# Projecting queries and keys behind the third value call of a turn, in a fused attention and FFN layer on one core

## The reference

```python
x = L0_attn_x                      # (32, 256, 128)
xn = _layernorm(x, axis=-1)
# attention: 16 heads of 8 channels
q = einsum('bsd,hde->bhse', xn, wq) + bq      # k and v in the same way
scores = softmax(einsum('bhse,bhte->bhst', q, k) * 8 ** -0.5)
att = einsum('bhst,bhte->bhse', scores, v)    # heads side by side again
attention = att @ wo.T + bo
# feed-forward, with the token before mixed in
xr = mu_r * xn + (1 - mu_r) * xn_prev         # xk in the same way
ffn = sigmoid(xr @ W_r.T) * (square(relu(xk @ W_k.T)) @ W_v.T)
return x + attention + ffn
```

## Time and profile before

| | us |
|---|---|
| median of 3 runs | 479.34 |
| lowest and highest run | 477.69, 480.9 |
| the profiled execution's own time | 477.82 |
| its span | 476.0 |

### The profile page before, as it was taken

The page is one execution under the profiler, slowest core; times in us unless marked ns, Lnnn a source line. Parts: engine busy times, 40 slices in busy tenths (PEclk is TensorE's granted clock), DMA queues, the critical chain, the costliest instruction groups (busy, mean ns, idle before and its releaser), DMA issues. The chain is left out here.

```text
span 476.0 us, 15644 instructions
## 1 busy us (share of the span) xinstructions
PE 444.1 (93%) x5238; PEld 272.0 (57%) x5238; DVE 402.4 (85%) x823; ACT 393.3 (83%) x866; POOL 367.9 (77%) x675
## 2 busy tenths in 40 slices
PE   5698999999999999999999999999999999999994
PEld 4244656565656656565666566566655565666541
DVE  7488898888989998899999888899998889988920
ACT  2047988989888898989888889898898898988883
POOL 6577888888878898788888888788897888876321
PEclk8579999999999999999999999999999999999998
DMA  4444355454344544453455454344554443445100
GB/s 142 134 125 125 104 147 157 127 147 141 111 122 145 156 141 138 121 145 113 127 154 149 139 148 124 102 142 135 156 154 124 149 127 111 129 135 147 47 15 22
DMA packets 85836, 60.42 MB, mean 127 GB/s; under 512 B 6192, under 2 KB 73392, under 8 KB 85808
## 3 DMA queue, kind: packets, MB, share of 16 engines
q1 hardware_dynamic: 85808, 60.06, 44.1%
HBM read 29.89 MB, written 29.36 MB: 124 GB/s over the span
## 5 line engine op out<-in xcount | busy, mean ns | idle before, releaser
L524 DVE TENSOR_REDUCE neg_max<-bank_max 128x2 f32<-128x512 f32 x512 | 328.2, 684 | 44.6 <-PE bank_max L645 40.1
L425 ACT ACTIVATE probs<-bank_exp 128x512 f32<-128x512 f32 x512 | 278.7, 600 | 25.4 <-PE bank_exp L635 24.1
L635 PE MATMUL bank_exp<-ops 51*128 51x256 bf16 x1024 | 156.9, 272 | 4.1 <-issue 3.0
L645 PE MATMUL bank_max<-ops 48*128 48x256 bf16 x1024 | 159.2, 276 | 0.0
L584 PE MATMUL bank_val<-probs,val 128*25 128x256 f32 x2048 | 138.1, 383 | 1.2 <-ACT probs L425 1.2
L635 PEld LDWEIGHTS bank_exp<-ops 51*128 51x128 bf16 x1024 | 75.0, 94 | 77.0 <-issue 65.2
L584 PEld LDWEIGHTS bank_val<-probs,val 128*25 128x25 f32 x2048 | 55.8, 103 | 41.6 <-issue 20.2
L645 PEld LDWEIGHTS bank_max<-ops 48*128 48x128 bf16 x1024 | 76.4, 95 | 5.2
L335 POOL TENSOR_SCALAR xn<-x_in,moments,rstd 128x128 f32<-128x128 f32 x62 | 49.4, 804 | 0.0
L374 POOL TENSOR_TENSOR mixed_x<-mixed_x,xn_t 128x512 f32<-128x512 f32 x32 | 40.7, 1272 | 2.5
L386 POOL TENSOR_TENSOR y<-projected,rest 128x256 f32<-128x256 f32 x32 | 23.4, 732 | 21.7 <-ACT projected L458 21.7
(11 more groups left out here) (67 smaller groups left out, 635.1 us busy)
## 6 DMA issues: line engine op xcount, KB each, us to landing
ops<-spill SPq DMA_DIRECT2D x128, 192.0 KB, 3.4
spill<-qk_h SPq DMA_DIRECT2D x64, 192.0 KB, 3.3
spill<-qk_m SPq DMA_DIRECT2D x64, 128.0 KB, 2.0
x_in<-x SPq DMA_DIRECT2D x32, 128.0 KB, 2.2
spill<-qk_l SPq DMA_DIRECT2D x32, 128.0 KB, 1.8
y_out<-y SPq DMA_DIRECT2D x32, 128.0 KB, 1.9
ops<-shift SPq DMA_DIRECT2D x128, 6.0 KB
w<-weights SPq DMA_DIRECT2D x1, 448.0 KB, 3.2
```

The costliest lines, as they stand in the source:

```text
L425: nc.scalar.activation(probs[g % 2][:, u % G, :, :], bank_exp[u % 2][:, :, :], ACT.Exp, scale=SCALE).then_inc(exp_done[u], 1)
L524: nc.vector.tensor_reduce(out=neg_max[hf][:, :, r, pr], in_=bank_max[MAX_BANK[v]][:, :, :], axis=AX_X, op=ALU.max, negate=True).then_inc(m ...
L635: exp_mm = nc.tensor.matmul(bank_exp[r][:, i, :], ops[p][rows, hf, 1, pr, i * P:(i + 1) * P], ops[p][rows, hf, 0, pr, :], start=True, stop ...
L645: max_mm = nc.tensor.matmul(bank_max[MAX_BANK[v]][:, i, :], of[rows, max_hf, 0, max_pr, i * P:(i + 1) * P], of[rows, max_hf, 1, max_pr, :] ...
```

## The change

The call of `project` moves from behind u 15 to behind u 13 of PE's program, directly behind value call 2. The key and query copies of ACT move from the head of the next turn to behind the exponential of u 13, so ahead of that of u 14, and name sample `t+3`. The ReLU `act_r` goes from behind the exponential of u 13 to behind that of u 11, after `projected`. DVE takes the keys' remainder behind the reduction of u 14, where it was u 15, and the queries' behind that of u 15, where it was u 1 of the next turn. As the copies are now in the turn of the projection, `near` and `far` swap in their calls. SP's and POOL's programs stay as they are.

```diff
--- before.py
+++ after.py
@@ -403,19 +403,16 @@
                 nc.scalar.copy(shift[half][:, :], shift_in_bank(bank)).then_inc(shift_done[half], 1)
 
             def move_qk(a, bank, n, moved):
-                act.wait_ge(qk_psum[a], n(2))
-                after(act, qk_rest_done[a], n(1))
+                act.wait_ge(qk_psum[a], n(3))
+                after(act, qk_rest_done[a], n(2))
                 if a == 1:
-                    after(act, spill_done, moved(1, SPILLS))
+                    after(act, spill_done, moved(2, SPILLS))
                 nc.scalar.activation(qk_h[:, a, :], bank[:, 0:S], ACT.Identity,
                                      bias=col[:, C_BQ + a:C_BQ + a + 1]).then_inc(h_done[a], 1)
 
             def step(t, c, n, moved, paired, quad, live):
                 p = c % 2
                 near, far = misc[p], misc[1 - p]
-                if live(2):
-                    move_qk(1, near, n, moved)
-                    move_qk(0, far, n, moved)
                 for u in range(H):
                     if live(0):
                         g = u // G
@@ -456,9 +453,12 @@
                         act.wait_ge(wo_psum, n(-1))
                         after(act, y_done, n(-2))
                         nc.scalar.copy(projected[:, :], near[:, 0:ST * D]).then_inc(wo_done, 1)
-                    if u == 13 and live(1):
+                    if u == 11 and live(1):
                         after(act, act_sq_done, n(0))
                         nc.scalar.activation(act_r[:, :], far[:, S:2 * S], ACT.Relu).then_inc(act_r_done, 1)
+                    if u == 13 and live(3):
+                        move_qk(1, far, n, moved)
+                        move_qk(0, near, n, moved)
 
             steps(act, step, (2, SPILLS))
 
@@ -523,10 +523,6 @@
                             after(dve, max_split[hf], n(ahead - 1))
                         nc.vector.tensor_reduce(out=neg_max[hf][:, :, r, pr], in_=bank_max[MAX_BANK[v]][:, :, :], axis=AX_X,
                                                 op=ALU.max, negate=True).then_inc(max_done[v], 1)
-                    if u == 1 and live(2):
-                        take_high(0, far, n(2), n(1))
-                        if not live(1):
-                            split_first()
                     if u == 5 and live(-1):
                         dve.wait_ge(tokens_psum, n(-1))
                         nc.vector.reciprocal(inv_den[:, :], by_head[:, :, E]).then_inc(inv_done, 1)
@@ -559,8 +555,12 @@
                         dve.wait_ge(weights_in, 16 * N_WEIGHT_DMAS)
                         dve.wait_ge(ident_made, 1)
                         fill_constants()
+                    if u == 14 and live(3):
+                        take_high(1, far, n(3), n(2))
                     if u == 15 and live(3):
-                        take_high(1, far, n(3), n(2))
+                        take_high(0, near, n(3), n(2))
+                        if not live(2):
+                            split_first()
 
             steps(dve, step, (SPILLS,))
 
@@ -724,7 +724,7 @@
                         last.then_inc(wo_psum, 1)
                     if u == 13 and live(0):
                         mix_values(2, n(0), n(-1), p)
-                    if u == 15 and live(3) and (live(1) or not live(2)):
+                    if u == 13 and live(3) and (live(1) or not live(2)):
                         project(c, n, live)
 
             steps(pe, step, (2,))
```

## The result

| | before | after |
|---|---|---|
| median, us | 478.51 (4 runs, 477.43 to 480.9) | 491.84 (4 runs, 491.14 to 493.56) |
| ratio, 95% interval | | 1.027 (1.023 to 1.032) |
| span of the profiled execution | 476.0 | 491.8 |

The change makes the kernel 2.7% slower, 13.3 us by the medians. The prediction was a loss of 8.6 us, 487.9 us in a range of 481.0 to 495.0.

A forecast was written before the change was run, and what follows sets the result against it. PE, busy 444.1 of 476.0 us, was taken to bound the kernel. Value call 2 to u 2 grows from 4.61 to 4.94 us; 0.33 x 29 = 9.6, less 1.0, gives 8.6 us: 487.9 us, range 481.0 to 495.0.

The forecast's parts named there:

- The stall on two exponential banks: At u 0 and 1, PE waits for the exponentials of u 14 and 15; u 14 to u 2 takes 2.96 us.
- The queries' copy: On ACT, it stands ahead of the exponential of u 14 and delays it by 0.09 us, bounds 0 and 0.25.
- the maxima's 0.05: At u 0 and 1, maxima matmuls, absent at the end of the trace, add 0.05 us behind the wait.
- The seams: On PE behind value call 2, joining the projection to the stretch saves 0.23 us a turn, 0.84 instead of 1.07.
- DVE's burst: Behind u 14, DVE takes maxima and remainders in a row; PE at u 3 and 4 barely doesn't wait.
- Rival C: DVE's run of work makes PE wait at u 3 or 4, 0.3 us a turn, 496.6 us; chance 0.06.
- The jumps: In six or seven turns where the loop jumps, 0.15 us each comes back before the transposes, 1.0 us.
- The ReLU: On ACT, it delays the exponentials of u 12 and 13 by about 0.35 us, off PE's path, costing nothing.
- POOL's vanished wait: POOL's wait for the remainders, 15.0 us in 28 turns, goes away but buys nothing, being off PE's path.
- Rival A: Milder stall at u 0 and 1, no delay by copies or maxima: 0.19 us a turn, 483.8 us; chance 0.20.
- Rival B: u 14, 15, 0 and 1 run through without waiting: 0.62 us a turn earlier, 461.3 us; chance 0.07.
- Rival D: PE's idle time at u 0 and 1 drops the granted clock to 1.2 GHz: 87 us, 575 us; chance 0.03.

The follow-up runs named there:

- The projection alone: Kernel before with PE's projection moved behind u 13 and the ReLU behind u 11, ACT's copies and DVE's remainders left in place: 507.97 us, 1.061 of before.
- the split: Changed kernel, but the queries' projection stays behind u 15, their copy and remainder in the next turn; the keys stay moved: 478.31 us, 0.998 of before.
- The repeated keys: Changed kernel with the keys' matmul done twice into the same place: 504.53 us in one execution.
- the square of four kernels: Changed kernel; with exponentials of u 14 and 15 halved (488.62 us); with DVE's remainder of the queries late (489.74 us); with both (481.62 us).

## Why the prediction was right, and where it was off

*The stall on two exponential banks* was the step that decided the sign, and it holds: u 0 came 1.17 and the transposes 1.93 behind u 14, where the end of the trace before had 1.17 and 1.89. The projection alone and the split show it from both sides. For u 14 to u 2, I had 3.10 and the chip 3.01. The queries' copy cost 0.05, not 0.09: the exponential starts 0.48 behind u 14 and u 0 1.17, where the kernel with the projection alone, without the copies there, has 0.43 and 1.12. Against the end of the trace before this is made up for by an answer of PE after 0.69 in place of 0.74. Of the maxima's 0.05, 0.04 show between u 0 and the transposes (0.76 against 0.72).

Some of the signs came out smaller than I wrote. PE is idle 0.55 before u 0, not about 0.7, and 16.5 us in all where I had 25 to 35; before u 1 its matmuls show no idle time of their own, and the wait stands in the weight loads (12.3 us).

*The seams* are the term that was mis-sized. The prediction took 0.23 as gained: keys 0.88 behind the value call and queries 0.43 behind the keys. The chip has 0.99 and 0.54, and what is gained is 0.02 (1.05 instead of 1.07). I had read 0.88 from a value call that is followed by the small bf16 transposes, and the 0.11 extra of the keys as the price of a change of kind. The upper bound (0.12 more) covered the first half of this error, but the second half had no bound. The repeated keys show that a full-array fp32 matmul pays the 0.11 behind a value call too. The weight loads of the changed kernel show where it is paid:

```profile
202.52 0.30 PEld L607 LDWEIGHTS misc<-xn_t,w 128*128 128x128 f32 x2 [0.42 <-issue]
202.84 0.41 PEld L610 LDWEIGHTS misc<-xn_t,w 128*128 128x128 f32 x2
```

The queries' load begins at 202.84, 0.22 ahead of their matmul at 203.06. The keys' load begins at 202.52 together with their matmul, after 0.42 us without a load, and the first of the two keys' matmuls lasts 0.48 in place of 0.38. The row that I took the 0.88 from has its load ahead: at 205.16 for the transposes at 205.38.

The Trainium skill (TensorE: Matmul & The Clock Gate, "Step-by-step: what each phase is for") says that weight loads are pulled ahead of matmuls in flight when their row groups don't conflict or the background buffer is their target. The trace shows that between keys and queries, and not between value call and keys. The sum by that rule had no gain from the seams, which is what came, but not for its reason: the seam is there, 0.54 against 0.43, in the changed kernel as before.

*DVE's burst* was called barely harmless; it costs 0.06 at u 3. Rival C was wrong about the size, but the square of four kernels shows that it is a full second limit just behind the first. The prediction didn't say what would follow if only the first were removed.

In sum: 0.33 + 0.21 (seams) - 0.09 (u 14 to u 2) + 0.06 (u 3) = 0.51 for a steady turn. *The jumps* give back 1 us as predicted: the turns after are equal, those before not. In microseconds over 29 turns: 8.6 + 6.1 - 2.6 + 1.7, less 1.4 for the two longer turns before, is 12.4. That the result stayed inside the range is in part luck: two of these terms go against the seams, and without them the loss is 16.4 us, which on the median of 479.34 ends at 495.7, past the 495.0. The rest of the turn didn't change. *The ReLU* is free, and POOL's vanished wait of 13 us bought nothing.

Rival A was the nearest of the others at u 0 to 2 and missed the seams as the forecast did. Rival B was excluded by the same rows that gave the forecast. Rival D didn't come: here is the changed kernel's stretch of two turns in the view by windows, with a granted clock of 1.00 in spite of the idle time.

```profile
200.00:228.30 28.30, 27.09 (x327) 16.40 (x326) 24.39 (x51) 24.74 (x55) 23.03 (x43) 1.00 0.47 131
```

The Trainium skill (TensorE: Matmul & The Clock Gate, "A second HAM failure mode: psum-queue depth-cycling") has micro-idles between groups swing the clock, in a kernel of 512-column bf16 matmuls. With idles of 0.55 us once a turn this case's trace doesn't show that in the steady turns.

## What to carry to other kernels

When matmuls of another kind stand between units that share few PSUM banks, they are the cover for the engine that empties these banks; count what is left between the last unit and the reuse of its bank before joining two stretches. Read a seam from a row with the same neighbours on both sides, since the same matmul cost 0.43 or 0.54 us by what stood ahead of it. When two engines limit the same place within some hundredths of a microsecond, shortening one gains nothing, and only a run with both shortened shows it.

## What was not expected of the hardware

A projection of 256 fp32 columns takes 0.43 us behind another full-array one, 0.54 behind a value call that uses 25-column tiles, and 0.63 to 0.64 when it stands alone between a stretch's two ends (210.85 to 211.48 and 212.02 to 212.66 in the split kernel). A value call takes 0.99 to 1.00 us to whatever followed it with 128 stationary columns, and 0.88 to the transposes with 24. Where these extra tenths fall, the first weight load of the new kind begins with its matmul, and where they don't it runs ahead by about 0.2 us. In these rows that goes with the shape and not with the number format: value call to keys is fp32 to fp32, from 25 columns to 128, and has no load ahead (202.52), while value call to transposes is fp32 to bf16, from 25 columns to 24, and has it (205.16 for 205.38). What holds the load back wasn't tested by a run of its own.
